# Returning expert outputs by scatter, scanning beside tiles, and squaring on DVE in a two-layer mixture-of-experts kernel

## The reference

```
x = layernorm(x + attention(x))          # 16 heads of 64, l2-normed q and k, softmax over 1024 keys
x = layernorm(x + moe_silu(x))           # 8 experts, top 2 of 8 by router logits
x = layernorm(x + state_space(x))        # depthwise convolution, then 16 linear recurrences
x = layernorm(x + moe_relu2(x))          # 8 experts top 2, plus one shared expert

moe_silu:  hidden = silu(x @ wg[e].T) * (x @ wu[e].T);   out += p[e] * (hidden @ wd[e].T)
moe_relu2: hidden = square(relu(x @ w_fc[e].T));         out += p[e] * (hidden @ w_proj[e].T)
state_space: dt = sigmoid(conv(x) @ dt_w.T + dt_b) * (0.1 - 0.001) + 0.001
             s[n] = exp(dt * A[n]) * s[n] + dt * conv(x) * b[n];   y = sum_n s[n] * c[n]
```

## Time and profile before

| | us |
|---|---|
| median of 3 runs | 1080.74 (1079.37 to 1081.22) |
| the profiled execution | 1075.24 |
| its span (what the trace covers) | 1073.5 |
| from the last result of a tile (ACT `yb`, 1034.35) to the end | 39.2 |

### The profile page before, as it was taken

How to read it: one execution, slowest core, us unless ns; L and a number is a source line. 1 busy time by engine, 2 the same in 40 slices (tenths; PEclk the granted TensorE clock), 3 DMA queues, 4 the chain that set the end, 5 groups by cost and what they waited for, 6 DMA issues and landing times. The chain is left out here.

```text
span 1073.5 us, 34731 instructions
## 1 busy us (share of the span) xinstructions
PE 913.9 (85%) x13676; PEld 858.4 (80%) x13676; DVE 728.1 (68%) x1463; ACT 770.0 (72%) x1275; POOL 501.1 (47%) x385
## 2 busy tenths in 40 slices
PE   4889999999999999999999951899969469899930
PEld 2778998999989989989999841899969359899830
DVE  6699988988998898889888744432459669410202
ACT  5689998988999889989988640544464266598831
POOL 5475755564655555555646116512328152043433
PEclk8799999999999999999999965899999689899975
DMA  8300000000000000000000041313201002023211
GB/s 263 113 2 6 18 3 22 3 3 22 3 3 22 3 22 3 3 23 3 2 22 2 2 177 38 103 54 86 54 26 30 3 28 70 11 68 97 61 55 42
DMA packets 43131, 42.13 MB, mean 39 GB/s; under 512 B 5600, under 2 KB 37344, under 8 KB 42848
## 3 DMA queue, kind: packets, MB, share of 16 engines
q1 hardware_dynamic: 38880, 31.51, 9.6%
q0 software_dynamic: 4096, 8.40, 2.7%
HBM read 25.60 MB, written 14.29 MB: 37 GB/s over the span
## 5 line engine op out<-in xcount | busy, mean ns | idle before, releaser
L557 ACT ACTIVATE Pr<-SC,cur_nesc,cur_esc 128x1024 f32<-128x1024 f32 x256 | 309.9, 1211 | 33.5 <-PE SC L417 17.0
L654 DVE TENSOR_TENSOR Pl<-Pr 128x1024 f16<-128x1024 f32 x224 | 287.5, 1302 | 44.8 <-ACT Pr L557 43.0
L416 PE MATMUL SC<-QK 128*128 128x256 f16 x1024 | 238.7, 274 | 1.0 <-ACT QK L539 1.0
L417 PE MATMUL SC<-QK 128*128 128x256 f16 x1024 | 238.6, 273 | 0.0
L442 PE MATMUL OP<-V,Pr 128*128 128x65 f16 x2048 | 214.4, 192 | 5.8 <-DVE Ob L676 5.7
L444 PE MATMUL OP<-V,Pr 128*128 128x64 f16 x2048 | 215.2, 195 | 0.0
L446 PE MATMUL OP<-V,Pl 128*128 128x65 f16 x2048 | 214.0, 191 | 0.0
L442 PEld LDWEIGHTS OP<-V,Pr 128*128 128x128 bf16 x2048 | 191.0, 97 | 12.5 <-issue 8.2
L444 PEld LDWEIGHTS OP<-V,Pr 128*128 128x128 bf16 x2048 | 190.0, 97 | 2.5
L446 PEld LDWEIGHTS OP<-V,Pl 128*128 128x128 f16 x2048 | 190.7, 99 | 0.0
L789 POOL TENSOR_TENSOR stk<-nrm,stk 128x512 f16<-128x512 f32 x64 | 75.2, 1175 | 147.6 <-DVE stk L636 147.6
(11 more groups left out here) (191 smaller groups left out, 2178.8 us busy)
## 6 DMA issues: line engine op xcount, KB each, us to landing
ys<-yb SPq DMA_DIRECT2D x92, 64.0 KB, 1.5
xg<-xs SPq DMA_DIRECT2D x12, 384.0 KB, 4.4
wst<-in_up SPq DMA_DIRECT2D x8, 512.0 KB, 3.5
xs<-zero SPq DMA_DIRECT2D x2, 1472.0 KB, 13.1
scratch<-in_up SPq DMA_DIRECT2D x1, 2304.0 KB, 8.2
wd<-in_wd SPq DMA_DIRECT2D x4, 576.0 KB, 10.7
wd<-in_wd SPq DMA_DIRECT2D x4, 512.0 KB
QK<-in_wqkv SPq DMA_DIRECT2D x4, 384.0 KB, 7.2
```

Of the source, the lines that this page charges most:

```text
L416: eng.matmul(out, QK[:, b, 1, key:key + P], rhs, start=True, stop=False)
L417: mm = eng.matmul(out, QK[:, b, 2, key:key + P], rhs, start=False, stop=True)
L557: eng.activation(Pr[:, n % PB, :, :], SC[s % 2][:, :, :], ACT.Exp, bias=cur_nesc[:, b:b + 1], scale=cur_esc[:, b:b + 1]).then_inc(s_exps, 1)
L654: eng.tensor_tensor(Pl[:, n % PB, :, :].rearrange("p a b -> p (a b)"), pr, high(pr)[:, 1::2], ALU.subtract).then_inc(s_low_probs, 1)
```

## The change

Four things are done.

1. **Return addresses.** A row in `xs` grows from 512 to 520 bytes: the number of the token that sent it and its first-choice expert. `choose` writes the expert, POOL the token number. `return_addresses` (DVE, two small instructions per six tiles) turns them into a row number per position: the token's first or second result, or a spare row for padding. `give_back` (POOL, one indirect DMA per tile) scatters `yb` straight to those rows of `ys`; `load_rows` (SP, four plain DMAs per phase) reads them back in token order. `store` and `gather` go. `xs` and `ys` exist once per phase instead of once per sequence; all four `xs` are cleared at the start, each with one DMA of zeros and one that writes a pad address into the last 8 bytes of each of its 2944 rows. `yb` has 12 buffers.
2. **Order of the scatters.** Seven of the 16 DMAs of scatter 1 stand ahead of the tiles, nine among the first of phase 0. Those of scatter 3 stand behind `give_back` of tiles 21 and 22 of phase 2 (`FREE_3` = TILES - 2), eight behind each. An inverse deviation (`NORM_3`) stands behind the third `give_back` of phase 2.
3. **Scans beside tiles.** The LayerNorm of sequence 0 moves to u = 33 (`TURN_1`), the convolution to 34, the step products to 36. From u = 38 on each tile has one scan on DVE, from 41 on one state product on PE, from 37 on a decay (two in the first) on ACT. From u = 37 on ACT applies Tanh, and DVE makes Silu times up from it in two instructions instead of one.
4. **Squares.** For u >= 77 ACT does Relu only, and DVE multiplies it by `AB`, which is the square.

```diff
@@ Constants.sync
-        eng.wait_ge(self.s_zero, 1)
-        for b in range(B):
-            eng.dma_start(t["xs"][b].rearrange("(j p) c -> p j c", p=P),
+        eng.wait_ge(self.s_zero, 4)
+        for rows in t["xs"]:
+            rows = rows.rearrange("(j p) c -> p j c", p=P)
+            eng.dma_start(rows[:, :, 0:2 * D],
                           t["zero"][:, :].unsqueeze(1).to_broadcast([P, TILES, 2 * D])).then_inc(self.s_cleared, 16)
+            eng.dma_start(rows[:, :, 2 * D:ROW], t["pad"][:, :, :].bitcast(F16)).then_inc(self.s_cleared, 16)
...
+ROW = 2 * D + 4
-YR = 8
+YR = 12
+FREE_1 = 7
+NORM_3 = 2
+FREE_3 = TILES - 2
+RETURN_2_AT = (9, 10, 11, 12)
+RETURN_AT = (1, 5, 11, 17)
-TURN_1 = SHARED_0 - 2
+TURN_1 = 33
+CONVOLVE_0 = TURN_1 + 1
+STEP_0 = TURN_1 + 3
+TANH_0 = STEP_0 + 1
+SCAN_0 = TANH_0 + 1
@@ sync
-            def store(ph, j):
...
+            def load_rows(ph, h):
+                for r in range(YR):
+                    wait(eng, s_y_stored[r], 16 * len(range(r, TILES * ph + TILES, YR)))
+                wait(eng, s_combined, 2 * TB * ph)
+                rows = ys[ph][0:2 * S].rearrange("(k i p) d -> p k i d", k=2, p=P)
+                for k in range(2):
+                    eng.dma_start(yg[:, k, 4 * h:4 * h + 4, :], rows[:, k, 4 * h:4 * h + 4, :]).then_inc(
+                        s_gathered[ph][h], 16)
@@ tensor
                     wait(eng, s_activated, u - 1)
+                    if u - 2 >= SHARED_1:
+                        eng.wait_ge(s_hidden, 2 * TILES + u - 2 - SHARED_1 + 1)
...
+                if u in (TURN_1, TURN_1 + 1):
+                    turn(1, 0, (u - TURN_1,))
+                if u == STEP_0:
+                    step_products(0)
+                if u < SHARED_0:
+                    for n in states_beside(u):
+                        state_products(0, n)
+            for n in range(SHARED_0 - SCAN_0 - 3, DS):
                 state_products(0, n)
@@ scalar
+                if u == TANH_0 - 1:
+                    sigmoids(0)
+                if u < SHARED_0:
+                    for n in decays_beside(u):
+                        decays(0, n)
@@ vector
+            def return_addresses(ph, c):
+                b, js = ph % 2, chunk_tiles(c)
+                eng.wait_ge(s_sorted_loaded[c], 16 * ph + 16)
+                eng.tensor_tensor(is_first[:, js], sender[:, js, 1], owner[:, b, js], ALU.is_equal)
...
+                eng.scalar_tensor_tensor(out=dest[:, b, js], in0=is_first[:, js], scalar=-float(S),
+                                         in1=sender[:, js, 0], op0=ALU.mult, op1=ALU.add).then_inc(s_dest, 1)
...
+                eng.scalar_tensor_tensor(out=h, in0=act[:, u % 2, :], scalar=1.0, in1=AB[u % 2][:, :], op0=ALU.add,
+                                         op1=ALU.mult).then_inc(s_gated, 1)
+                eng.wait_ge(s_gated, u - TANH_0 + 1)
+                eng.scalar_tensor_tensor(out=h, in0=h, scalar=0.5, in1=UB[u % 2][:, :], op0=ALU.mult,
+                                         op1=ALU.mult).then_inc(s_hidden, 1)
+            def square(u):
+                eng.wait_ge(s_activated, u + 1)
...
+                eng.tensor_tensor(hid[:, u % HR, :], act[:, u % 2, :], AB[u % 2][:, :], ALU.mult).then_inc(s_hidden, 1)
...
+            for u in range(SHARED_1, UNITS):
+                square(u)
+                if SHARED_1 <= u - LAG2 < SPARSE_3:
+                    add_shared(u - LAG2)
+                if 0 <= u - SPARSE_3 - 2 < CHUNKS:
+                    return_addresses(3, u - SPARSE_3 - 2)
+                for h in range(2):
+                    if u == SPARSE_3 + 6 + 2 * h:
+                        combine(2, h)
+                        statistics(3, 0, (h,))
+                if u == SPARSE_3 + 13:
+                    shifts(3, 0)
@@ gpsimd
+            def give_back(ph, j):
+                J = TILES * ph + j
+                eng.wait_ge(s_dest, CHUNKS * ph + j // CHUNK + 1)
+                eng.wait_ge(s_down_read, J + 1)
+                eng.indirect_dma_start(
+                    out=ys[ph], out_offset=bass.IndirectOffsetOnAxis(ap=dest[:, ph % 2, j:j + 1], axis=0),
+                    in_=yb[:, J % YR, :], in_offset=None).then_inc(s_y_stored[J % YR], 16)
...
-            scatter(1, -3)
-            gather(0, 25)
+            scatter(1, range(FREE_1))
+            for j in range(TILES):
+                give_back(0, j)
+                if FREE_1 + j < 2 * TB:
+                    scatter(1, (FREE_1 + j,))
...
-            inverse_deviations(2, 1)
-            scatter(3, 64)
-            gather(2, SPARSE_3 + 1)
+            for j in range(TILES):
+                give_back(2, j)
+                if j == NORM_3:
+                    inverse_deviations(2, 1)
+                if j >= FREE_3:
+                    scatter(3, range(8 * (j - FREE_3), 8 * (j - FREE_3) + 8))
```

More of the change, by code:

```diff
@@ L1656, in inverse_deviations, with scatter @@
                                       ALU.pow).then_inc(s_rstd, 1)
-            def scatter(ph, first=None):
+            def scatter(ph, pieces=range(2 * TB)):
                 b = ph % 2
-                eng.wait_ge(s_slots, ph + 1)
-                eng.wait_ge(s_split_low, ph + 1)
-                for k in range(2):
-                    for i in range(TB):
-                        if first is not None:
-                            wait(eng, s_gate_products, first + TB * k + i)
-                        eng.indirect_dma_start(
-                            out=xs[b], out_offset=bass.IndirectOffsetOnAxis(ap=slots[:, b, k, i:i + 1], axis=0),
-                            in_=split[:, b, i, :], in_offset=None).then_inc(s_scattered[ph], 16)
```

200 lines of the change are left out of this document (118 added, 82 removed).

## The result

Time: 1091.26 us, median of four runs (1089.79 to 1092.07), beside 1080.22 for the kernel before in runs taken together with it. The ratio is 1.0101, 95% interval 1.0085 to 1.0117: slower by 11.0 us, where 2.2 us faster was forecast and 1089 was the end of the range. The profiled execution after took 1092.07 (span 1090.2); that of before 1075.24 (span 1073.5) lay 5.0 under the 1080.22, and that of after 0.8 above its own median, so the two traces differ by 16.7 us. The table splits these 16.7 at the same places of both traces.

The account below looks back on a forecast made before the run. DVE was taken to bound sequence 0's scans, and chains of waits at POOL's DMAs phase 0's start and the end. Terms -14.5 - 10.3 + 17.9 + 3 + 0.4 + 1.3 = -2.2 us gave 1078.5 us median, range 1069 to 1089.

Parts of the forecast that it names:

- the small terms: Phase 2's inverse deviation, return addresses, phase 0's copy and longer rows: +1.3 us, 0 to 3; other give_backs hide beside tiles.
- Scans beside tiles: Sequence 0, from step 38 to the add behind the scans: the add comes 10.3 us earlier, at 827.2 against 837.5.
- Phase 3's wait: Ahead of phase 3's first transposes: eighteen POOL DMAs bring its rows late, +17.9 us, between 17 and 19.5.
- The end: Behind T, the end of the last yb: first combine at T + 5.9, second at T + 9.4, before T + 23.9; -14.5 us.
- Clock and tiles of phase 3: PE at half clock after phase 3's wait, +3 us (0 to 4); phase 3's tiles, +0.4 (-2 to +3).
- The squares: Phase 3's tiles: Square off ACT wins 1.4 and 0.6 more, two combines among DVE's squares cost 2.5; sum +0.4 us.
- The start: Zero and pad DMAs ahead of the first wst load in SP's queue: 0 us, from 0 to +20.
- Pads: Rival, chance 0.13: at ACT's first w0h, pads hold up attention from 43 ns a piece; at 60 ns 12.5 us, 1091.
- Serial steps: Rival, chance 0.07: steps 41 to 45 don't overlap, 7.8 us instead of 4.25 each, 17.8 more: 1096; half of it 1087.
- Longer rows: Rival, chance 0.05: scatters of 520-byte rows in phases 0 and 3 take half as long again, +19 us, 1098.
- Hidden scatter: Rival, chance 0.04: PE does not stand at phase 3, the scatter is hidden; sum -23 us, 1057.
- More overlap in the scans: Rival, chance 0.08: scans of sequence 0 reach DVE's floor, no clock loss; -2.7 - 3 more us, 1073.

Follow-up runs that it names:

- the fourth series: The last four experiment runs, on a chip of their own with their own runs of the kernel before; the changed kernel measured 1083.78 us there, ratio 1.0059.
- the pair of kernels in the fourth series: The changed kernel unchanged (1083.78 us) and the changed kernel with sequence 0's scans behind the tiles again (1091.56 us).
- both hybrids: Changed kernel with paced DMAs, clears behind first loads, and return by scatter in phases 0 and 1 (1070.06 us), or phase 3 as well (1062.58 us).
- e3: Changed kernel with phase 3's scatters two at a time behind give_backs 5 to 12 of phase 2; 1094.09 us, ratio 1.0131.
- e10: e8 with the inverse deviation of sequence 0's LayerNorm behind phase 1's give_back 16 instead of 5; 1083.93 us, ratio 1.0079.
- e2: Changed kernel with the last nine scatter DMAs of phase 1 one behind every second give_back; 1094.75 us, ratio 1.0155.
- e8: Changed kernel with scans, decays, state products, LayerNorm, convolution and step products of sequence 0 behind the tiles again; 1108.02 us, ratio 1.0265.
- e13: The changed kernel unchanged, run again in the fourth series; 1083.78 us, ratio 1.0059.
- e15: e10 unchanged, run again in the fourth series; 1091.56 us, ratio 1.0136.
- e1: Kernel before without the gate-product waits in scatter(1) and, but for the first, scatter(3); 512-byte rows; 1113.27 us, ratio 1.0321.
- the third: The series of four experiment runs just before the fourth series, on its own chip with its own runs of the kernel before; e10 measured 1083.93 us there.

## Why the prediction was wrong

**The step that failed** is the sentence on the small terms: "The other `give_back`s, one per tile at 1.3 us against steps of 1.79 and 2.44, hide beside tiles; in phase 0's first nine steps POOL has two per step and falls back by some us, which 12 buffers of `yb` take up." POOL did fall back and the buffers did take it up; no wait came from that. But I counted only POOL's own time. Back to back, its indirect DMAs stop PE: 13.3 us in phase 0 and 5.2 beside the wait of phase 3, 18.5 in all, against 0. Take them away and the traces differ by 16.7 - 18.5 = -1.8, where the sum said -2.2; so close only because the unforeseen 4.1 at the end (below) makes up for what came later elsewhere, which is luck. In the trace of before, the longest run of DMAs beside tiles at that distance is four, so no row showed it. The traces' 16.7 is 5.7 more than the medians' 11.0, since the profiled execution before was a quick one and that of after a slow one; which terms hold these 5.7 isn't known, but the steps of the tiles show the stops directly. In the fourth series the stops were smaller (from tile 0 to 15 of phase 0 it took 43.6 us, 8.4 more than before, instead of 13.3 more), and so was the loss, 6.0 in medians.

**The terms of the sum.** Scans beside tiles: right, -9.8 and, by the pair of kernels in the fourth series, -8.8 to -9.5 (forecast -10.3). Phase 3's wait: right, +18.7 where it stands without stops (forecast +17.9). The end: -13.3 up to the second combine, against -14.5; the term that was mis-sized is the start of the first, T + 7.2 where I had T + 5.9: 1.0 of it because tile 21's `give_back` still stood ahead of tile 22's, 0.4 in SP's waits and the load (3.8 where I had 3.4). The other -4.1 was not forecast: what followed was to be "the same". The stretch from the last LayerNorm to the span's end, in which the profile shows only the output's transfer, is 7.7 to 8.4 us in before, the kernels made from it and both hybrids, and 4.2 to 4.6 in eight of the nine traces of the changed kernel and its variants (7.8 in the one with `scatter(1)` behind every second `give_back`). What makes the difference no row shows. Clock and tiles of phase 3: +1.1 instead of +3.4, and +4.3 without stops; in the trace after, the shared tiles ran until 1012.66, so PE did not start from rest: the 0.50 of the earlier trace rows fell on them, and from 1014 it is 1.00. The squares: nothing, as said. The start: +3.8 instead of +0.5. ACT's wait for `wst` is 3.0 us in that trace, but the same kernel started its tiles at 675.31 without that wait, 0.4 behind before: no cost of the start is shown.

**The rivals.** Pads: the sign that it named, a wait of ACT for `wst` near 80 us, came, at 3.0 and not 12.5, but its condition did not: the pieces took 24 to 38 ns, not over 43. Zeros of 6.6 to 8.0 us instead of 4.4 took the rest of the room. Of the other kernels with the clears ahead of the first load of `wst`, `e3` and `e10` have waits of 1.29 and 0.58 in their traces, `e2`, `e8`, `e13` and `e15` have none. Serial steps: refuted, 4.19. Longer rows: refuted, 0.96 for rows of 520 and of 512 bytes alike, and e1 has stops with short rows. Hidden scatter: refuted by 18.22. More overlap in the scans: not seen, the steps keep PE's 4.18. None of them, nor the range, had an engine that loses time to another's DMAs without a wait between them; the result lies 2.3 us above the range.

**Open.** What PE and POOL share. The profile names `issue` and `remote`, no engine of this core; the DMA engines moved little, 0.16 to 0.22 of their time. Why one of the five series (the result's and the four of the experiments), the third, was free of stops at 1.26 isn't known either, nor why the zeros took 6.6 to 8.0 us.

## What to carry to other kernels

When a change hands more indirect DMAs to GpSimd, count the distance between them as well as their sum: here 1.67 us apart they cost PE nothing and 1.26 apart, in four series of five, up to about 1 us each, though a scatter for a later phase shares no buffer and no semaphore with PE's tiles. Waits that pace a queue to the tiles may be what keeps another engine running; before they go, take them out alone and measure. And a move that frees the end of a kernel by filling a queue in its middle is best taken in the phases in which that queue has room, and left out in the others (here phase 2, whose surplus would hold up phase 3).

## What the runs showed of the hardware

- 32 indirect DMAs (0.96 us of POOL each, 28 of them beside busy tiles) at 1.26 us cost 34 and 34 us in two series; at 1.46, 23 us in another; at 1.67, nothing (in a third series; another kernel at 1.67 had no stops in a series with them). PE's matmuls then start one or two per DMA, and its completions reach ACT and DVE late (a transpose of 677.87 was taken at 692.35); the hand-overs from ACT to DVE and to PE don't show it. In the densest case it sets in 5 us after PE starts beside the run and is gone 4 us after the start of its last DMA.
- It isn't in every series: in one of five, 19 DMAs stood at 1.26 beside tiles and PE was busy for 24.00 of 24 us.
- DMA pieces of 8 bytes into HBM, 184 for each DMA engine, took 4.4 to 7.0 us with other packets among them, 24 to 38 ns a piece, where the small loads of the earlier trace rows took 18. The Trainium skill, "DMA: Bandwidth & Descriptors", Specifications, has transfers under 512 bytes read, modify and write; the trace agrees in direction, and doesn't show the reason.
- Some of the indirect DMAs beside tiles took 1.2 to 1.45 us of POOL instead of 0.96; before, those beside the scans of sequence 0 mostly took 1.88.
